# GpSimd takes the norm scalars, the weight quantisation and the split maxima of a four-layer gated transformer

## The chip, the core and the metric

The kernel runs as one program on one core of a Trainium2 chip. Its five engines run side by side and meet at semaphores: TensorE (PE: matrix products and transposes into the eight PSUM banks), VectorE (DVE), ScalarE (ACT), GpSimd (POOL, which also issues the indirect DMAs) and SyncE (SP, which issues most DMAs). The metric is the time of one execution on the device in microseconds, lower is better.

## The reference

Thirty-two positions `b` of 128 tokens and 128 channels pass four layers. Each layer adds an attention onto a context, and then a feed-forward part, both gated by a tanh and both fed with a layer norm of `x`:

```python
x = x + tanh(g_xattn[0]) * L0_xattn(_layernorm(x), ctx, ctx, ...)      # 16 heads of 8, biases
x = x + tanh(g_ffn[0])   * L0_ffn(_layernorm(x), w1, w2)               # bit-linear, gelu
x = x + tanh(g_xattn[1]) * L1_xattn(_layernorm(x), ctx, ctx, mask)     # one head of 128
x = x + tanh(g_ffn[1])   * L1_ffn(_layernorm(x), w_gate, w_up, w_down) # bit-linear, gated silu
x = x + tanh(g_xattn[2]) * L2_xattn(_layernorm(x), ctx, ctx, ...)      # 16 heads, shared key and value
x = x + tanh(g_ffn[2])   * L2_ffn(_layernorm(x), ...)                  # 8 experts, one per token
x = x + tanh(g_xattn[3]) * L3_xattn(_layernorm(x), ctx, mask, ...)     # 16 heads, masked
x = x + tanh(g_ffn[3])   * L3_ffn(_layernorm(x), ...)                  # butterfly transforms of 512

def _layernorm(x, eps=1e-05):
    m = mean(x); v = var(x)
    return (x - m) / sqrt(v + eps)

def _quant_weight(w):                                # both bit-linear layers, five weights in all
    s = clip(mean(abs(w)), EPS, None)
    return clip(round(w / s), -1.0, 1.0) * s         # used as it is; activations go to 8 bits
```

The attentions run along `b`-and-token pairs that the layouts in the kernel turn into 32 tiles of 128 rows; a softmax over 128 keys is taken for each of the 16 heads, with its true maximum.

## The kernel before

All of `x` stays in SBUF as 32 tiles of 128x128. The phases follow each other: attention L0, bit-linear F0, attention L1, bit-linear F1, attention L2, experts F2, attention L3, butterfly F3. Every engine has its own program, written out in the order in which it runs; no scheduler moves anything. An attention with 16 heads is a software pipeline over `t`: at iteration `t` PE makes the scores of tile `t` in both orientations (`pair_of_scores`, L1045 and L1048), DVE takes the maxima of tile `t+2` (L1487, two per tile), and ACT the exponentials (L753). The maxima of a tile are split into three bf16 parts (`nmax_parts`), transposed by PE (L1112), and subtracted again through a matrix product (L1517, L1059). In the attentions named in `SPLIT_BY_POOL` the four operations of that split are GpSimd's (`split_maxima`, L629 to L635), in the others DVE's (L1534, L1536, L1544, L1556). Four tiles are a quad; for each quad ACT writes normed tiles (`xn_quad`, L815), PE transposes them (L1123) and projects queries, keys and values (L1174, L1132, L1181), and ACT and DVE write copies masked to one head (`one_head_keys`, `one_head_queries`).

A norm has two stages. `tile_stats` (L1402) leaves the statistics of each tile in `stats` as soon as that tile of `x` is done. Between two phases DVE's `norm_stats` (L1410 to L1424) makes `mean`, `rstd` and `shift` for all 32 tiles at once, with a square root on ACT (`root`, L720) in the middle. Then the next phase's first `xn` can be written (L815, L858 or L1429). GpSimd has its own version, `norm_of` (L563 to L572), which takes the root as a power; it is used at the start of L0 and, quad by quad, for the routing.

Before either bit-linear phase DVE quantises its weights (`quantised_weights`, L1606 to L1617): for each weight a sum of magnitudes, a mean over the partitions by PE, a scale, and three passes over 128x512. PE then transposes the weights and DVE copies them (L1624) before the first tile can be quantised (L1641).

While L2 attends, the routing of F2 runs beside it. For each quad GpSimd makes the norms (L563 to L572) and the normed tiles (`late`, L659), PE transposes one tile per iteration (L1106) and makes the logits, DVE finds each token's expert and its rank, GpSimd adds the starts (L665 to L669) and scatters the four tiles to the experts' rows in HBM with four indirect DMAs in a row (`scatter`, L681). After L2 come the last quads' routing, F2 (its results go back with 40 indirect DMAs, L695), and then the residual additions (L1822) and statistics in four parts of eight tiles. `fill_wait` (L957) puts matrix products whose result nobody reads in front of a wait.

During L3 GpSimd multiplies butterfly matrices (`butterfly_step`, L614 and L619), three or four steps after each split.

## Time and profile before

| | |
|---|---|
| Median of 3 runs | 1155.06 us (1154.85 to 1159.28) |
| Profiled execution | 1164.92 us, its span 1163.2 us |
| PE, DVE, ACT, POOL busy in the span | 80%, 68%, 59%, 29% |
| Mean granted clock of PE | 0.904 |
| L0 / F0 / L1 / F1 | 0 to 250 / to 330.6 / to 386 / to 490 us |
| L2 / rest of the routing and F2 / residual | to 728 / to 850 / to 870 us |
| L3 / F3 | to 1092.5 / to 1163 us |

A row of a timeline gives the start, the busy time and the engine, then the line, the operation and its shape, "xN" for N instructions merged, and in brackets how long the engine sat idle before it and what ended that. SPq is the queue in which SP issues DMAs. "remote" is a release that the profile can't place.

### The profile page before, as it was taken

Reading aid. Unit: us, or ns where it says so; the run is one execution under the profiler, and the core shown is the slowest. Engines: PE = TensorE matmul, PEld = TensorE weight load, DVE = VectorE, ACT = ScalarE, POOL = GpSimd, SP = SyncE. Lnnn points to the kernel's source line nnn. Section 1 sums busy time; section 2 is a strip of 40 time slices with the busy share of each in tenths; the row PEclk is TensorE's granted clock in tenths of the full one; section 3 lists DMA queues with packets and bytes.
Section 4 is the critical chain, followed back from the end, with each engine's and each line's share of the span. In section 5 each row is a group of like instructions: output and inputs, shape, how many; then the busy total and the mean of one; then the engine's idle time right before and its main releaser. Section 6 shows DMA issues by size and latency. Waiting matters only on the chain.

```text
span 1163.2 us, 28810 instructions
## 1 busy us (share of the span) xinstructions
PE 934.0 (80%) x9421; PEld 556.2 (48%) x9431; DVE 786.8 (68%) x2141; ACT 688.1 (59%) x1474; POOL 334.5 (29%) x692
## 2 busy tenths in 40 slices
PE   3888998946656366599999986499929999999899
PEld 3644444423444233334554443277713454544598
DVE  3567777758989899848887872345583666667444
ACT  3556666528855466467777642065516777775466
POOL 5411111100000000001133344434413998777000
PEclk9999999976679677699999995599969999999899
DMA  6987655469995200000000000112130111111011
GB/s 181 157 108 52 49 42 43 37 152 202 181 180 76 72 1 1 1 1 2 2 10 12 11 18 21 31 54 57 56 100 19 57 39 56 54 52 47 3 34 36
DMA packets 285280, 67.04 MB, mean 58 GB/s; under 512 B 206241, under 2 KB 277985, under 8 KB 285154
## 3 DMA queue, kind: packets, MB, share of 16 engines
q1 hardware_dynamic: 279394, 50.94, 28.2%
q0 software_dynamic: 4896, 14.18, 3.7%
q8 instruction: 77, 1.26, 0.5%
q10 hardware_dynamic: 864, 0.27, 0.2%
q14 instruction: 49, 0.40, 0.1%
HBM read 34.80 MB, written 30.56 MB: 56 GB/s over the span
## 4 chain that ended last, share of the span: by engine, by line
PE 54%; DVE 28%; issue 6%; ACT 3%; DMA 3%; POOL 2%; SPq 1%; DVEq 1%; another core or an unknown queue 1%; ACTq 0%; POOLq 0%
PE bank L1045 14%; DVE nmax L1487 8%; PE bank L1077 6%; PE bank L1151 3%; PE bank L1333 3%; PE bank L1318 3%; DVE small L1661 3%; PE bank L1365 3%; PE bank L1059 2%; PE bank L1373 2%; DVE stats L1402 2%; DVE q_one L1653 2%; PE bank L1048 2%; DVE q_one L1690 2%; PE bank L1035 2%
## 5 line engine op out<-in xcount | busy, mean ns | idle before, releaser
L1487 DVE TENSOR_REDUCE nmax<-bank 128x8 f32<-128x1024 f32 x192 | 234.7, 1223 | 144.0 <-PE bank L1048 139.7
L753 ACT ACTIVATE probs_space<-bank 128x1024 f32<-128x1024 f32 x192 | 196.5, 1023 | 139.8 <-PE bank L1059 138.9
L1045 PE MATMUL bank<-q_one,k_all 32*128 32x512 f32 x768 | 216.8, 633 | 29.5 <-DVE nmax L1487 25.9
L1048 PE MATMUL bank<-k_one,q_all 32*128 32x512 f32 x768 | 214.2, 631 | 2.5 <-DVE nmax L1487 1.1
L1077 PEld LDWEIGHTS bank<-probs_space,vals 128*32 128x32 f32 x3072 | 73.6, 110 | 122.2 <-issue 121.6
L1077 PE MATMUL bank<-probs_space,vals 128*32 128x128 f32 x3072 | 126.3, 281 | 0.0
L563 POOL TENSOR_TENSOR var_b<-stats 128x4 f32<-128x4 f32 (+2 forms) x12 | 2.5, 208 | 356.7 <-DVE stats L1402 355.7
L1045 PEld LDWEIGHTS bank<-q_one,k_all 32*128 32x128 f32 x768 | 62.2, 185 | 58.6 <-issue 54.7
L761 ACT ACTIVATE k_one<-k_all,one_head 128x512 f32<-128x512 f32 x96 | 68.8, 722 | 20.1 <-DVE k_all L1507 18.6
L1059 PE MATMUL bank<-nmax_one,ones_bf 12*128 12x512 bf16 x384 | 78.1, 379 | 0.0
L1517 DVE TENSOR_TENSOR nmax_one<-bank,max_row 128x512 bf16<-128x512 bf16 x96 | 65.4, 681 | 3.6 <-PE bank L1112 3.6
L922 ACT ACTIVATE q_one<-bank,moe_b 128x128 f32<-128x128 f32 x160 | 45.8, 369 | 37.0 <-PE bank L1326 30.3
L629 POOL CAST nmax_parts<-nmax 128x16 bf16<-128x16 f32 x64 | 12.7, 198 | 184.5 <-DVE nmax L1487 184.4
L1402 DVE BATCH_NORM_STATS2 stats<-x 128x6 f32<-128x128 f32 x232 | 60.7, 286 | 5.9 <-DMA x<-in_x_dram 3.3
L957 PE MATMUL bank<-ones_bf 128*128 128x512 bf16 x125 | 38.4, 440 | 29.8 <-DVE stats L1402 24.0
L1048 PEld LDWEIGHTS bank<-k_one,q_all 32*128 32x128 f32 x768 | 58.7, 184 | 5.6 <-issue 4.5
L695 POOL DMA_INDIRECT token_rows<-q_one,slot_row_int x40 | 38.7, 967 | 64.7 <-DVE q_one L1800 64.3
L614 POOL TENSOR_TENSOR late<-bf_up,late 128x512 f32<-128x512 f32 x36 | 56.8, 1598 | 0.0
L1541 DVE RECIPROCAL o_inv<-bank 128x16 f32<-128x16 f32 x96 | 24.5, 255 | 44.5 <-PE bank L1156 36.6
L767 ACT ACTIVATE q_one<-q_all,one_head 128x512 f32<-128x512 f32 x80 | 54.5, 726 | 0.0
L875 ACT ACTIVATE q_one<-bank 128x1024 bf16<-128x1024 f16 x32 | 32.8, 1023 | 30.6 <-PE bank L1244 30.6
L942 ACT ACTIVATE q_one<-bank,up_bias 128x128 f32<-128x128 f32 x128 | 36.5, 368 | 18.7 <-PE bank L1365 18.7
(287 smaller groups left out, 2198.2 us busy)
## 6 DMA issues: line engine op xcount, KB each, us to landing
expert_rows<-zeros SPq DMA_DIRECT2D x8, 2128.5 KB, 32.0
late<-in_L_ffn_up_weights_dram POOLq DMA_DIRECT2D x9, 512.0 KB, 4.1
late<-_L_ffn_down_weights_dram POOLq DMA_DIRECT2D x9, 512.0 KB, 4.1
q_one<-expert_rows SPq DMA_DIRECT2D x40, 64.5 KB
q_scratch<-late SPq DMA_DIRECT2D x8, 256.0 KB
v_scratch<-moe_w SPq DMA_DIRECT2D x8, 256.0 KB, 3.1
vals<-v_scratch SPq DMA_DIRECT2D x8, 256.0 KB, 7.3
o_scratch<-o_tok SPq DMA_DIRECT2D x32, 64.0 KB, 3.4
```

What stands on the lines that cost most here:

```text
L614: pool.tensor_tensor(tmp(i), half(src, i % 2), weight, ALU.mult).then_inc(S("bf_step"), 1)
L753: act.activation(probs[:, 2 * g:2 * g + 2, :, :].rearrange("k g i q -> k (g i q)"), bank_pair[1][:, :, :].rearrange("k g f -> k (g f)"), A ...
L761: act.activation(k_one[:, c % 2, i, :], k_all[:, c % 2, :], ACT.Copy, scale=one_head[:, i:i + 1]).then_inc(S("t_k1"), 1)
L767: act.activation(q_one[:, c % 2, i, :], q_all[:, c % 2, :], ACT.Copy, scale=one_head[:, i:i + 1]).then_inc(S("t_q23" if i >= 2 else "t_q01 ...
L922: m = act.activation(hid2[:, t % 2, c * P:(c + 1) * P], bank[2 + t % 2][:, c * P:(c + 1) * P], ACT.Gelu_apprx_tanh, bias=moe_b1[:, bass.ds ...
L1045: pe.matmul(bank[2 + s], group(k_all, u, 2 * g + s), group(q_one, u, 2 * g + s), start=not masked, stop=False)
L1048: m = pe.matmul(bank[s], group(q_all, v, 2 * f + s), group(k_one, v, 2 * f + s), start=not masked, stop=True)
L1059: m = pe.matmul(bank[2 + s], ones_bf[first:last, :], nmax_one[first:last, u % 2, :, :], start=False, stop=True)
L1077: m = pe.matmul(bank[4][32 * j:32 * j + 32, g * P:(g + 1) * P], v[:, first:first + VW], probs[:, 2 * g + j // 2, j % 2 * 2 + s, :], start= ...
L1402: dve.bn_stats(stats[:, u, :], x[:, u * P:(u + 1) * P]).then_inc(S("stats"), 1)
L1487: dve.tensor_reduce(nmax[:, u % 2, 0, :].rearrange("q (g i) -> q g i", i=HG)[:, 2 * g:2 * g + 2, :], bank_pair[0][:, :, :].rearrange("q g ...
L1517: dve.tensor_tensor(nmax_one[:, (t + 1) % 2, :, :], over_blocks(bank[6][:, 3 * P:4 * P].bitcast(BF16)[:, 0:P], HG), max_row[:, :].unsqueez ...
```

## The change

1. `norm_stats` and `root` go. GpSimd's `norm_of` makes `rstd` and `shift` for groups of tiles, (0,8), (8,24), (24,32), and (0,4), (4,16), (16,32) for L3. Each user of a normed tile waits for the semaphore `norms` up to its tile.
2. The five bit-linear weights are loaded during L0 (`later_weights`, three more transfers), summed by DVE at the end of L0's iterations 10 to 14, scaled at 16, and quantised by GpSimd after its splits 19 to 23, three passes over 128x512 each.
3. In L2 too GpSimd splits the maxima, and two of the four `one_head_queries` of a quad move from DVE to ACT. Its routing work is spread over the iterations: norms of quad `c` after split `4c+8`, starts after `4c+14`, one scatter per iteration from 15 on.
4. L2's iterations -10 to -3 run between the last pairs of F1 on PE and ACT. The first quad uses bank 2, the fills go to bank 3, and L2's fills ahead of its first quads (9, 3, 3, 3) go. L3's start fill, 12 long, begins at the first residual addition.
5. Residual additions and statistics ahead of L3 come in parts (0,4), (4,8), (8,16), (16,24), (24,32), and L3's keys masked to one head wait for the first halves of them (`B_res`).

```diff
-        SPLIT_BY_POOL = ("L0", "L3")
-        STATS_BEFORE = {"L2": 5, "L3": 7}
-        NORMS = {"L2": 4, "L3": 5}
+
+        SPLIT_BY_POOL = ("L0", "L2", "L3")
         X_LEAD = 10
+
+        NORMS = {"F0": 0, "L1": NT, "F1": 2 * NT, "L2": 3 * NT, "L3": 4 * NT, "F3": 5 * NT}
+
+
+        SIZES_FROM, SCALES_IN, QUANTISED_FROM = 10, 16, 19
+
+        TENSOR_BETWEEN = {12: range(-X_LEAD, -5), 13: (-5,), 14: (-4, -3)}
+        SCALAR_BETWEEN = {11: range(-X_LEAD, -6), 12: (-6, -5), 13: (-4, -3)}
...
             def later_weights():
...
+                for i, name in enumerate(("L0_ffn_w1", "L0_ffn_w2", "L1_ffn_w_gate", "L1_ffn_w_up", "L1_ffn_w_down")):
+                    if i in (1, 4):
+                        sp.dma_start(quant_src[:, i, :], A[name]).then_inc(S("w_quant"), 16)
+                    else:
+                        sp.dma_start(quant_src[:, i, :].rearrange("p (c d) -> p c d", d=P),
+                                     A[name].rearrange("(c p) d -> p c d", p=P)).then_inc(S("w_quant"), 16)
...
+                if keep_scale:
+                    link(pool.tensor_tensor(var_a[:, at], var_a[:, at], keep[:, at], ALU.mult))
                 link(pool.tensor_scalar(rstd[:, at], var_a[:, at], 2.0, 0.0, ALU.mult, ALU.add), False)
                 link(pool.tensor_tensor(shift[:, at], mean2, var_a[:, at], ALU.mult))
+
+            def norms(stats_before, first, last, keep_scale=False):
+                pool.wait_ge(S("stats"), stats_before + last)
+                norm_of(first, last - first, keep_scale)
+                pool.sem_inc(S("norms"), last - first)
...
                     split_maxima(2 * NT, v)
+                    if v == 16:
+                        norms(7 * NT, 0, 8)
                     for _ in range(3 if k < 6 * STAGES else 4):
                         if k < 12 * STAGES:
                             butterfly_step(k)
                             k += 1
+                norms(7 * NT, 8, 24)
+                norms(7 * NT, 24, NT)
+
+            def quantised_weight(i):
+                own, inverse = quant_src[:, i, :], quant_inv[:, i:i + 1]
+                pool.wait_ge(S("wscale"), 1)
+                link(pool.tensor_scalar(own, own, inverse, MAGIC, ALU.mult, ALU.add))
+                link(pool.tensor_scalar(own, own, -MAGIC, 1.0, ALU.add, ALU.mult))
+                pool.tensor_scalar(quant_bf0[:, i, :] if i < 2 else quant_bf[:, i - 2, :], own, 1.0, -1.0,
+                                   ALU.min, ALU.max).then_inc(S("wq_ready"), 1)
 
             for v in range(NT):
                 split_maxima(0, v)
+                if v == 16:
+                    norms(NT, 0, 8)
+                if 0 <= v - QUANTISED_FROM < 5:
+                    quantised_weight(v - QUANTISED_FROM)
+            norms(NT, 8, 24)
+            norms(NT, 24, NT)
+            for layers in (2, 3, 4):
+                for first, last in ((0, 8), (8, 24), (24, NT)):
+                    norms(layers * NT, first, last)
             if "F2" in phases:
                 def norm_of_quad(c):
                     pool.wait_ge(S("stats"), NT * 5 + QT * (c + 1))
@@ -669,25 +701,32 @@
                     link(pool.tensor_tensor(dest[:, c % 2, :, :], dest[:, c % 2, :, :], hot[:, c % 2, :, :], ALU.mult))
                     pool.sem_inc(S("R_start"), 1)
 
-                def scatter(c):
+                def numbered(c):
...
                                    channel_multiplier=1, allow_small_or_imprecise_dtypes=True))
-                    pool.wait_ge(S("R_dest"), c + 1)
-                    for t in range(QT * c, QT * c + QT):
-                        pool.indirect_dma_start(
-                            out=expert_rows, out_offset=bass.IndirectOffsetOnAxis(ap=dest_int[:, t:t + 1], axis=0),
-                            in_=ring[:, t % ROUTE_RING, :], in_offset=None).then_inc(S(f"scattered_{c % 4}"), 16)
-
-                for c in range(NQ + 1):
-                    if c < NQ:
+
+                def scatter(t):
+                    pool.wait_ge(S("R_dest"), t // QT + 1)
+                    pool.indirect_dma_start(
+                        out=expert_rows, out_offset=bass.IndirectOffsetOnAxis(ap=dest_int[:, t:t + 1], axis=0),
+                        in_=ring[:, t % ROUTE_RING, :], in_offset=None).then_inc(S(f"scattered_{t // QT % 4}"), 16)
+
+                for v in range(NT + 4 * QT):
+                    if v < NT:
+                        split_maxima(NT, v)
+                    c = (v - 8) // QT
+                    if v % QT == 0 and live(c, NQ):
                         norm_of_quad(c)
-                    if c >= 1:
-                        rows_of_quad(c - 1)
-                        scatter(c - 1)
+                    c = (v - 14) // QT
+                    if v % QT == 2 and live(c, NQ):
+                        rows_of_quad(c)
+                        numbered(c)
+                    if live(v - 15):
+                        scatter(v - 15)
...
+            pool.wait_ge(S("wT_out"), 2)
+            for first, last in ((0, 4), (4, 16), (16, NT)):
+                norms(6 * NT, first, last, keep_scale=True)
...
                         past(act, "t_s1", 2 * (tiles + QT * (c - 1)))
+                        if layer == "L3" and c < 2:
+                            act.wait_ge(S("B_res"), (c + 1) * NT // 2)
...
+                        act.wait_ge(S("norms"), NORMS[layer] + u + 1)
                         act.activation(xn_quad[:, u % QT, :], x[:, u * P:(u + 1) * P], ACT.Identity,
                                        bias=shift[:, u:u + 1], scale=rstd[:, u:u + 1]).then_inc(S("t_xn"), 1)
...
+                    if next_iteration is not None and j in SCALAR_BETWEEN:
+                        if j == min(SCALAR_BETWEEN):
+                            act.wait_ge(S("bit_qx"), 2 * NP)
+                        for t in SCALAR_BETWEEN[j]:
+                            next_iteration(t)
...
-                    pe.wait_ge(S("stats"), NT * STATS_BEFORE[layer])
-                    if masked:
-                        pe.wait_ge(S("masks"), 1)
-                    fill_wait(9)
+                if layer == "L3":
...
+                    pe.wait_ge(S("B_res"), 1)
+                    fill_wait(12)
+
+                def quad_bank(c):
+
+                    return bank[2] if own and c == 0 else bank[5]
...
-                for t in iterations(layer):
+                def iteration(t):
                     u, w = t - lag, t - R_XT
                     routed = layer == "L2" and live(w)
+                    if layer == "L2" and t == -6:
+                        pe.wait_ge(S("bit_ge"), 2 * 2 * NP)
+                    if layer == "L2" and t == -3:
+                        pe.wait_ge(S("bit_hm"), 2 * NP)
+                    if layer == "L2" and t == 0:
+                        pe.wait_ge(S("stats"), NT * 5)
...
-                        if own and c == 0:
-                            fill_wait(3)
+                        if masked and c == 0:
+                            fill_wait(3, 3)
...
+                    if next_iteration is not None and j in TENSOR_BETWEEN:
+                        for t in TENSOR_BETWEEN[j]:
+                            next_iteration(t)
...
-            def norm_stats(n, n_stats=None, scale_by_keep=False):
-
-                dve.wait_ge(S("stats"), NT * (n_stats or n))
-                link(dve.tensor_tensor(var_a[:, :], stats[:, :, 2], stats[:, :, 5], ALU.add))
...
-                dve.sem_inc(S("var"), 1)
...
-                dve.sem_inc(S("norm"), 1)
-
             def normed(dst, u, name):
-                dve.tensor_scalar(dst, tile_of(x, u), column(mean, u), column(rstd, u), ALU.subtract,
-                                  ALU.mult).then_inc(S(name), 1)
+                wait(dve, "norms", NORMS[name.partition("_")[0]] + u + 1)
+                dve.tensor_scalar(dst, tile_of(x, u), column(rstd, u), column(shift, u), ALU.mult,
+                                  ALU.add).then_inc(S(name), 1)
...
+                    if not own and t == SCALES_IN:
+                        dve.wait_ge(S("wmean"), 1)
+                        link(dve.tensor_scalar(quant_scale[:, :], bank[7][:, P:P + 5], EPS, None, ALU.max))
+                        dve.reciprocal(quant_inv[:, :], quant_scale[:, :]).then_inc(S("wscale"), 1)
...
+                    i = t - SIZES_FROM
+                    if not own and 0 <= i < 5:
+                        dve.wait_ge(S("w_quant"), 16 * 5)
+                        link(dve.tensor_reduce(quant_sum[:, i:i + 1], quant_src[:, i, :], AX.X, ALU.add,
+                                               apply_absolute_value=True))
+                        if i == 4:
+                            dve.sem_inc(S("wsum"), 1)
...
-                dve.wait_ge(S("w_f0"), 32)
-                link(dve.memset(quant_sum[:, :], 0.0))
-                quantised_weights((0, 2), 1)
-                norm_stats(2)
                 bit_ffn("F0", False, 4)
...
-                for c in range(NT // GC):
-                    dve.wait_ge(S(f"chunk_in{c}"), 32)
-                    for t in range(c * GC, (c + 1) * GC):
+                for first, last in ((0, QT), (QT, GC), (GC, 2 * GC), (2 * GC, 3 * GC), (3 * GC, NT)):
+                    dve.wait_ge(S(f"chunk_in{first // GC}"), 32)
+                    for t in range(first, last):
                         dve.scalar_tensor_tensor(out=x[:, t * P:(t + 1) * P], in0=shared[:, t * P:(t + 1) * P],
                                                  scalar=gate[:, t:t + 1], in1=x[:, t * P:(t + 1) * P],
                                                  op0=ALU.mult, op1=ALU.add).then_inc(S("B_res"), 1)
-                    dve.wait_ge(S("B_res"), (c + 1) * GC)
-                    for t in range(c * GC, (c + 1) * GC):
+                    dve.wait_ge(S("B_res"), last)
+                    for t in range(first, last):
                         tile_stats(t)```

PE's program at the end of F1, first before and then of the change. L1226 (now L1300) is the last product of a pair of F1, L1244 (L1318) its transposes; `xn_quad`, `l_wq`, `l_wkv` and `k_one` are L2's.

```order
L1226 MATMUL bank<-ffn_wT,q_one 128x128 x8
L1244 MATMUL bank<-ident_half,q_one 128x128 x8
L1226 MATMUL bank<-ffn_wT,q_one 128x128 x8
L957 MATMUL bank<-ones_bf 128x512 x9
L1123 MATMUL bank<-ident,xn_quad 128x128 x4
L957 MATMUL bank<-ones_bf 128x512 x3
L1174 MATMUL bank<-xnT_quad,l_wq 128x512
L957 MATMUL bank<-ones_bf 128x512 x3
L1132 MATMUL bank<-contextT,l_wkv 128x512
L957 MATMUL bank<-ones_bf 128x512 x3
L1181 MATMUL bank<-l_wkv,contextT 128x128 x4
```

```order
L1300 MATMUL bank<-ffn_wT,q_one 128x128 x8
L1318 MATMUL bank<-ident_half,q_one 128x128 x8
L1186 MATMUL bank<-ident,xn_quad 128x128 x4
L1241 MATMUL bank<-xnT_quad,l_wq 128x512
L1300 MATMUL bank<-ffn_wT,q_one 128x128 x8
L1318 MATMUL bank<-ident_half,q_one 128x128 x8
L1195 MATMUL bank<-contextT,l_wkv 128x512
L1300 MATMUL bank<-ffn_wT,q_one 128x128 x8
L1248 MATMUL bank<-l_wkv,contextT 128x128 x4
L1004 MATMUL bank<-ones_bf 128x512 x8
L1101 MATMUL bank<-k_one,q_all 128x512 x2
```

The transposes and the query and key projections of L2's first quad now stand ahead of the last pairs of F1, and 18 fills are gone.

GpSimd's program in L2, between the norms of one quad and those of the next, before and then of the change (L659 and L691 write the normed tiles, L681 and L714 are the scatters, L640 to L646 the split):

```order
L571 TENSOR_SCALAR rstd<-var_a 128x4
L572 TENSOR_TENSOR shift<-twice_mean,var_a 128x4
L659 TENSOR_SCALAR late<-x,rstd,shift 128x128 x4
L665 COPY late<-late 128x8
L667 TENSOR_TENSOR late<-late 128x8 x4
L668 TENSOR_TENSOR late<-late 128x32
L669 TENSOR_TENSOR late<-late,hot 128x32
L677 IOTA late 128x4
L681 DMA expert_rows<-late,dest_int 33792x129 x4
L563 TENSOR_TENSOR var_b<-stats 128x4
```

```order
L577 TENSOR_SCALAR rstd<-var_a 128x4
L578 TENSOR_TENSOR shift<-twice_mean,var_a 128x4
L691 TENSOR_SCALAR late<-x,rstd,shift 128x128 x4
L714 DMA expert_rows<-late,dest_int 33792x129
L640 CAST nmax_parts<-nmax 128x4x4
L642 TENSOR_TENSOR nmax<-nmax,nmax_parts 128x16
L644 CAST nmax_parts<-nmax 128x4x4
L646 TENSOR_TENSOR nmax_parts<-nmax,nmax_parts 128x4x4
L714 DMA expert_rows<-late,dest_int 33792x129
L640 CAST nmax_parts<-nmax 128x4x4
L642 TENSOR_TENSOR nmax<-nmax,nmax_parts 128x16
L644 CAST nmax_parts<-nmax 128x4x4
```

The four scatters in a row have become one after each split, and the norms of a quad stand behind a split.

## Rows read from the trace of the kernel before

**Rows 1.** The page: share of the chain that ended last, by engine.

```profile
PE 54%; DVE 28%; issue 6%; ACT 3%; DMA 3%; POOL 2%; SPq 1%; DVEq 1%; another core or an unknown queue 1%; ACTq 0%; POOLq 0%
```

**Rows 2.** L3: busy time of PE, PEld, DVE, ACT, POOL; then DVE's maxima.

```profile
885.00:1085.00 200.00, 190.47 (x2954) 98.44 (x2954) 130.08 (x214) 140.59 (x237) 157.33 (x252) 1.00 0.13 44
...
L1487 DVE TENSOR_REDUCE nmax<-bank 128x8 f32<-128x1024 f32 x64 | 78.4, 1224 | 67.8 <-PE bank L1048 64.6 <-POOL nmax_parts L635 1.6 <-POOL nmax_parts L629 1.6
```

**Rows 3.** DVE's timeline from L0 into F0 (see above for its columns).

```profile
250.11 1.41 DVE L1606 TENSOR_REDUCE quant_sum<-late 128x1 f32<-128x512 f32 x2
...
257.77 0.76 DVE L1624 COPY ffn_wT<-bank 128x512 bf16<-128x512 bf16 x2 [0.15 <-DVE shift L1424]
```

**Rows 4.** DVE's timeline from F0 into L1.

```profile
330.62 0.22 DVE L1410 TENSOR_TENSOR var_a<-stats 128x32 f32<-128x32 f32 x1
...
333.09 0.60 DVE L1429 TENSOR_SCALAR xn<-x,mean,rstd 128x128 f32<-128x128 f32 x2
```

**Rows 5.** DVE's timeline from L1 into F1.

```profile
386.02 2.11 DVE L1606 TENSOR_REDUCE quant_sum<-late 128x1 f32<-128x512 f32 x3
...
395.70 1.09 DVE L1624 COPY ffn_wT<-bank 128x512 bf16<-128x512 bf16 x3 [0.15 <-DVE shift L1424]
```

**Rows 6.** PE's timeline from F1 into L2.

```profile
490.26 3.69 PE L957 MATMUL bank<-ones_bf 128*128 128x512 bf16 x9 [1.19 <-DVE stats L1402]
...
503.22 1.13 PE L1048 MATMUL bank<-k_one,q_all 32*128 32x512 f32 x4 [0.58 <-issue]
```

**Rows 7.** Waits in L2 (505 to 728): total us, times, longest us.

```profile
PE bank L1045 <- DVE nmax L1487: 12.1, 22, 1.7
...
DVE o_inv L1541 <- remote: 7.9, 4, 2.5
```

**Rows 8.** GpSimd's timeline in L2: the norms of a quad and its normed tiles.

```profile
624.00 0.21 POOL L563 TENSOR_TENSOR var_b<-stats 128x4 f32<-128x4 f32 x1 [2.28 <-DVE stats L1402]
...
627.48 1.75 POOL L659 TENSOR_SCALAR late<-x,rstd,shift 128x128 f32<-128x128 f32 x4
```

**Rows 9.** DVE's and PE's timelines in the same iteration of L2.

```profile
626.38 1.22 DVE L1487 TENSOR_REDUCE nmax<-bank 128x8 f32<-128x1024 f32 x1 [0.35 <-PE bank L1048]
...
630.78 0.27 PE L1106 MATMUL bank<-ident,late 128*128 128x128 f32 x1
```

**Rows 10.** All 40 of F2's returning indirect DMAs: min/median/max ns, start.

```profile
L695 POOL DMA_INDIRECT token_rows<-q_one,slot_row_int x40: 962/966/988, 760.3 to 848.3; - x40
```

**Rows 11.** GpSimd's timeline at the end of the routing: first and last of the late scatters.

```profile
732.32 1.10 POOL L681 DMA_INDIRECT expert_rows<-late,dest_int  x1 [0.94 <-DVE dest_int L1584]
...
744.32 0.97 POOL L681 DMA_INDIRECT expert_rows<-late,dest_int  x1 [0.30 <-issue]
```

**Rows 12.** DVE's and ACT's timelines ahead of L3, and GpSimd's power by size.

```profile
864.74 1.64 DVE L1402 BATCH_NORM_STATS2 stats<-x 128x6 f32<-128x128 f32 x8
...
875.68 0.49 ACT L815 ACTIVATE xn_quad<-x,shift,rstd 128x128 f32<-128x128 f32 x1 [1.21 <-PE bank L1123]
...
L570 POOL TENSOR_TENSOR var_a<-var_b,minus_half x12: 1017/1170/2269, 12.6 to 725.0; 128x4 f32<-128x4 f32 x9, 128x8 f32<-128x8 f32 x2, 128x12 f32<-128x12 f32 x1
```

**Rows 13.** GpSimd's timeline in L3.

```profile
992.90 0.20 POOL L629 CAST nmax_parts<-nmax 128x16 bf16<-128x16 f32 x1 [1.30 <-DVE nmax L1487]
...
993.91 1.55 POOL L614 TENSOR_TENSOR late<-bf_up,late 128x512 f32<-128x512 f32 x1
```

**Rows 14.** The chain of waits in L0, and SP's queue ahead of it.

```profile
94.22 4.10 SPq L407
...
60.36 4.58 SPq L377 DMA_DIRECT2D late<-in_L_ffn_w_dram  x1
64.99 0.50 SPq L379 DMA_DIRECT2D late<-in_L_ffn_w_dram  x1
```

**Rows 15.** DVE's timeline in L0: first maximum of two iterations that follow.

```profile
133.04 1.22 DVE L1487 TENSOR_REDUCE nmax<-bank 128x8 f32<-128x1024 f32 x1 [1.40 <-PE bank L1048]
...
138.30 1.23 DVE L1487 TENSOR_REDUCE nmax<-bank 128x8 f32<-128x1024 f32 x1 [0.75 <-PE bank L1048]
```

## What the change does to the time: the prediction

> **What bounds the kernel.** I read the page first, for who carries the chain: PE 54% and DVE 28%, and GpSimd 2% [rows 1]. So the kernel is a relay between PE and DVE. An instruction taken from DVE counts where the chain runs through DVE, and GpSimd is the engine with room. Then I read how full the stretches are. In L3 PE is busy 190.47 us of 200, GpSimd 157.33 [rows 2]: there GpSimd has little room left. Last I read the timelines of the five seams between phases, where DVE alone works and PE is idle [rows 3 to 6, 12], and the waits and GpSimd's timeline in L2 [rows 7 to 11].
>
> **L0 to F0: +7.3 us.** DVE begins the sums of the weights at 250.11 and reaches the copy of the transposed weights at 257.77 [rows 3]: 7.66 us of quantising and norms that all go. PE's transposes of the two weights and the last group's norm on GpSimd were hidden beside this and are now bare. I take 0.4 off, and keep 6 to 8.
>
> **F0 to L1: +0.5.** The norms take 333.09 - 330.62 = 2.47 us [rows 4], which go. But in L1 each of DVE's 32 tiles now waits for `norms` against a register before its `xn`. The trace has no such wait. DVE is the engine without a pause there, and by the smallest gaps between its instructions I put 0.06 us on each, 2 us in all. The ends are 0 and 0.1 us on each, so this seam gives between -0.7 and +2.5.
>
> **L1 to F1: +8.7.** The same as into F0, with three weights: 395.70 - 386.02 = 9.68 [rows 5], less 1.0 for three transposes that now stand alone. Between 8 and 9.7.
>
> **F1 to L2: +10.** Before, nine fills of 0.41 each begin only at 490.26, when the last statistics are there. The whole chain of quad 0 follows, and the first scores start at 503.22 [rows 6]. Now transposes and both projections of quad 0 stand ahead of the last products of F1. After the last product (1.19 before 490.26, so 489.1) PE has only the values' projection (0.6) and eight fills (8 x 0.41 = 3.3) to go, and starts scores at about 493.0. That is 10.2. The moved instructions have to fit into waits of PE and ACT between the last pairs; for what doesn't I take 0.2, and at worst 3. Between 7 and 11.
>
> **Inside L2: +3.5, the least certain term, made of three.**
> - DVE has four fewer operations in each tile and two fewer in each quad. PE's scores waited for DVE's maxima 22 times, 12.1 us in all [rows 7]. I take 7.5 of it, since the maxima themselves (1.22 each, two a tile) stay. Between 0 and +12.
> - Four times DVE waited for something that the profile can't place, 7.9 us in all, 2.5 at the longest [rows 7]; I found each of these beside the last of four scatters in a row, with PE and ACT idle as well. Spread out, the bursts are gone. F2 issues 40 single indirect DMAs of 962 to 988 ns each [rows 10]. I take +8, with 0 as the lower end and, for the case that every scatter brings such a wait, the first rival below.
> - The norms of a quad now stand behind a split on GpSimd. After the maximum of that iteration ends GpSimd needs 1.0 for the split (992.90 to 993.91, [rows 13]), 3.48 for the norms (624.00 to 627.48) and 0.44 for the first of four tiles [rows 8]: 4.9 us. PE asks for this tile in the next iteration, 630.78 - (626.38 + 1.22) = 3.2 us after the maximum [rows 9]. PE's instructions run in order, so everything behind L1106, the scores included, is late by 1.7, or 2.0 with the hops between the engines. Six quads have it while maxima run: -12. Between 0 (if the earlier relief is eaten up by this, the two overlap) and -15.
>
> **End of the routing: +3.** The last eight scatters took from 732.32 to 745.3 (744.32 + 0.97), in two bursts with the last quad's starts between them [rows 11]. The order at the end changes little, but normed tiles and starts are ready earlier. Between 0 and +7.
>
> **Into L3: +6.5.** Parts of eight tiles take 3.81 us on DVE, and the third ended at 866.38 [rows 12], so tile 16's statistics are there at 862.6. GpSimd needs for (4,16) about 2.31 (the 3.48 of four tiles less their power, 1.17) and 2.27 for the wider power [rows 8, 12]: 867.2. ACT wrote the first tile of the second quad at 875.68 [rows 12]; it can be 8 earlier. The key masks wait for 16 and 32 residual additions, which moves part of it back. Between 4 and 9.
>
> **GpSimd's norms in the middle of L3: -2.3.** At split 16 eight tiles' norms come in, about 3.9 us (3.48, and up to 0.5 for the wider power). GpSimd had at best 1.30 us of slack before a split [rows 13]. The rest, 2.6, delays a split, hence PE's L1112. Between -3 and 0. In L0 the same norms fit: a period is 138.30 - 133.04 = 5.26 us [rows 15], and a split and they take 4.9.
>
> **L3 to F3: +1.** The norms, 2.47 as in rows 4, go, but PE and ACT have weights of their own to prepare there. Between 0 and 2.5.
>
> **Loads and sums in L0: -4.5.** SP issues three more transfers ahead of the rows of L0 that it has to return. The two there took 4.58 and 0.50 us [rows 14], so three take 1.5 to 9.7. SP's issue of those rows is on the chain (L407, 4.10 at 94.22, [rows 14]). I take -2.5, nearer to the 0.50, since the 4.58 also holds a wait for a place in the queue. DVE's five sums cost 0.70 each (2.11 for three, [rows 5]), 3.5 in all; DVE sits idle 1.40 and 0.75 before its maxima [rows 15], which hides a part: -2, between -3.5 and 0. GpSimd's quantising is three passes over 512 columns; a pass lies between 0.44 (128 columns, [rows 8]) and 1.55 (two operands of 512 columns, [rows 13]), so 1.3 to 4.7 us behind a split of 1.0, in a period of 5.26. It is hidden, or at the upper end 0.4 too long five times.
>
> Against all work moved to GpSimd stands this: in L3, with GpSimd busy four fifths of the time, DVE's maxima last 1224 ns [rows 2], and 1.22 in L2 and L0 [rows 9, 15]. The Trainium skill (GPSIMD Engine Reference, Specifications) states that GpSimd shares its interfaces to SBUF with VectorE and that the two contend when DVE's instruction has two SBUF inputs. The maxima read PSUM, so this trace neither bears it out nor refutes it; by that rule each of the 15 passes of the quantising could hold DVE up once in L0, at most 15 x 1.55 = 23 us. Few of DVE's instructions in L0 have two inputs in SBUF, and no price for it is in the sum.
>
> **Sum.** 7.3 + 0.5 + 8.7 + 10 + 3.5 + 3 + 6.5 - 2.3 + 1 - 4.5 = 33.7 us. The profiled execution would fall from 1164.92 to 1131.2. That execution lies 9.86 above the median; taken off the median of 1155.06 the forecast is 1121.4, say 1122.
>
> **Rivals.**
> 1. *Slower: each scatter brings the unplaced wait.* If it comes of an indirect DMA's issue beside the pipeline and not of four in a row, 17 single scatters run inside L2's loop. At 2.5 each (the longest in rows 7) they cost 42.5, and the time is 1121.4 + 42.5 = 1164. It decides from 2.0 us a scatter. For: it appeared only beside scatters. Against: the wait came once for four of them, and F2's 40 single ones keep a steady length [rows 10]. 5%.
> 2. *GpSimd is late more often.* Its order is fixed, so a late norm delays splits, and a late split delays PE. If the stall on the normed tile costs 4 rather than 2 us (-12), and the loads in L0 cost 6.5 rather than 2.5 (-4), 1138. For: GpSimd goes from 2% of the chain to a link in each iteration of L2, and two waits for it show in L3 already [rows 2]. Against: it was busy only 29% of the whole span. 20%.
> 3. *More gain: the stall on the normed tile is not there.* PE asks for it 3.2 us after the maximum only in an iteration that runs undisturbed; if PE is behind anyway the 4.9 fit in: +12, 1110. 20%.
> 4. *No change.* Rival 1 at 2.0 us each, or rivals 1 and 2 in part: 1155. 3%.
>
> **How the numbers follow.** The forecast's case has 52%, its own range 1113 to 1131. For 8 in 10 the range takes in most of rivals 2 and 3, whose terms reach -12 and +12 and a few us more: 1103 to 1142. What a measurement can tell from no change is 0.5%, 5.8 us. Faster by more than that is 52 + 20 + 20 = 92%, within it 3%, slower 5%.
>
> **What the profile after would show.** Right: DVE goes from L0's last statistics to the weights' copy with no other work between; scores of L2 start within 4 us of F1's last product; no "remote" wait in L2; in its place PE's transpose of the normed tile (L1106 before) waiting for GpSimd some 2 us, six times; in L3 one late split near tile 16; the first masked maxima about 6 us sooner after the last residual. Wrong: "remote" waits at each scatter (rival 1); waits of PE for `nmax_parts` in L2 and a gap in L0's rows near 90 us (rival 2); no wait of that transpose (rival 3). The forecast fails if the seams give their 33 us but L2 itself becomes longer than before by more than 10.

## The result: 1167.6 us, slower, and the profile after

The change is slower, by 0.9%. Its median is 1167.6 us (1160.07 to 1174.18, 13 runs) against 1156.51 (1153.25 to 1161.19, 13 runs); the ratio is 1.0091, 95% interval 1.0066 to 1.0116. The forecast was 1122, its range 1103 to 1142, with 5% on slower.

The page of the changed kernel, its second section and the chain by engine, which answers to [rows 1]:

```profile
PEclk9998999995578777799998885589988999999999
...
PE 51%; DVE 22%; POOL 10%; issue 8%; ACT 3%; DMA 3%; SPq 2%; DVEq 1%; ACTq 0%; POOLq 0%
```

GpSimd has gone from 2% of the chain to 10%. DVE lost what it was meant to lose, 28% to 22%. PE's clock, in tenths of full speed by slice, falls to 8 in the second half of L2 (the three 8s in a row), where the kernel before has 9s throughout L2.

To see where the time went, I cut both executions at the starts of the first and the last maximum of each attention with 16 heads (DVE's line L1487, now L1542; 64 in each). "Half clock" is the time within the part at which PE had 1.2 GHz instead of 2.4.

| part | before, us | after, us | difference | forecast | half clock before / after |
|---|---|---|---|---|---|
| up to L0's first maximum | 52.1 | 52.6 | +0.5 | 0 | |
| L0 | 175.8 | 188.2 | +12.4 | +4.5 | 0 / 20 |
| L0's end, F0, L1, F1, L2's start | 276.5 | 249.4 | -27.1 | -26.5 | 140 / 140 |
| L2 | 190.5 | 215.7 | +25.2 | -3.5 | 0 / 27 |
| routing's end, F2, L3's start | 190.4 | 186.3 | -4.1 | -9.5 | 75 / 82 |
| L3 | 189.7 | 191.4 | +1.7 | +2.3 | 0 / 0 |
| rest of L3, F3 | 88.1 | 84.6 | -3.5 | -1.0 | 7.5 / 0 |
| span | 1163.2 | 1168.3 | +5.1 | -33.7 | |

(The difference of the medians is 11.1. The profiled execution of before lay 8.4 above its median, that of after 2.4, which is the other 6.)

Each part is read from one execution. How far such a reading carries shows in the kernels below that leave a part as it is in the change: L0 took 182.3 to 191.6 us in eight executions, with 7 to 31 us at half clock, and L2 212.5 to 222.3 in five, with 22 to 42. L3, with its full clock, took 191.2 to 191.7 in ten.

The seams gave what was forecast. First DVE's timeline of the changed kernel from L0 into F0, and then PE's from F1 into L2:

```profile
262.61 0.29 DVE L1477 BATCH_NORM_STATS2 stats<-x 128x6 f32<-128x128 f32 x1
262.82 0.74 DVE L1673 COPY ffn_wT<-bank 128x512 bf16<-128x512 bf16 x2
```

```profile
484.64 0.62 PE L1300 MATMUL bank<-ffn_wT,q_one 128*128 128x128 bf16 x8
485.59 1.13 PE L1248 MATMUL bank<-l_wkv,contextT 128*128 128x128 f32 x8 [0.34 <-ACT k_all L820]
486.56 1.89 PE L1004 MATMUL bank<-ones_bf 128*128 128x512 bf16 x8
488.97 1.13 PE L1101 MATMUL bank<-k_one,q_all 32*128 32x512 f32 x4 [0.52 <-issue]
```

The weights' copy follows the last statistics at once, where 7.66 us lay between them [rows 3]. L2's first scores start 3.7 us after F1's last product has ended (485.3); before it was 14.1 (489.1 to 503.22, [rows 6]).

The loss is inside L2 and L0. The waits from 490 to 735 us in the changed kernel (total, times, longest), to be read against [rows 7]:

```profile
PE bank L1098 <- DVE nmax L1542: 15.6, 18, 2.2
...
PE bank L1169 <- POOL late L691: 10.6, 6, 2.4
...
DVE late L1642 <- POOLq L702: 8.4, 5, 1.7
```

The second row is the wait I had forecast: six times, 1.8 on average. The third I had not. PE never waits here for `nmax_parts`, and no unplaced wait is left in L2. Here is one of each, PE's timeline of one quad, and DVE's:

```profile
645.97 2.05 PE L1248 MATMUL bank<-l_wkv,contextT 128*128 128x128 f32 x8
...
656.10 0.33 PE L1164 MATMUL bank<-ident,o_tok 128*128 128x128 f32 x1
658.06 0.46 PE L1169 MATMUL bank<-ident,late 128*128 128x128 f32 x1 [1.64 <-POOL late L691]
658.31 0.31 PE L1175 MATMUL bank<-ident_bf,nmax_parts 128*128 128x128 bf16 x1
658.42 2.02 PE L1195 MATMUL bank<-contextT,l_wkv 128*128 128x512 f32 x2
```

```profile
641.07 0.19 DVE L1642 TENSOR_REDUCE late<-late 128x4 f32<-128x32 f32 x1 [1.69 <-POOLq L702]
641.29 0.17 DVE L1643 CAST dest_int<-late 128x4 int32<-128x4 f32 x1
641.37 1.23 DVE L1542 TENSOR_REDUCE nmax<-bank 128x8 f32<-128x1024 f32 x1
```

DVE's L1642 adds up the rows of a quad, and it waits for the starts that GpSimd now makes behind a split. The next maximum stands behind it in DVE's order, and PE's scores behind that:

```profile
642.74 0.66 PE L1098 MATMUL bank<-q_one,k_all 32*128 32x512 f32 x1 [2.23 <-DVE nmax L1542]
```

After this wait and after the one at 658.06 PE works at half speed: the key projection at 658.42 takes 2.02 us, where it took 1.08 before. Two rows of PE's timeline of the kernel before, the second of them that projection:

```profile
177.06 0.66 PE L1045 MATMUL bank<-q_one,k_all 32*128 32x512 f32 x1 [1.50 <-DVE nmax L1487]
...
630.94 1.08 PE L1132 MATMUL bank<-contextT,l_wkv 128*128 128x512 f32 x2
```

Busy time and clock of three stretches of the changed kernel (duration, then PE, PEld, DVE, ACT, POOL, then the granted clock), the first while GpSimd is late, the second behind that wait, and the third behind an earlier wait of 2.24 us at 584.51:

```profile
655.00:658.00 3.00, 1.43 (x23) 0.51 (x17) 1.74 (x5) 1.31 (x3) 2.49 (x8) 1.00 0.00 0
658.50:661.80 3.30, 3.30 (x12) 1.04 (x12) 0.69 (x1) 1.66 (x4) 1.90 (x3) 0.54 0.09 25
```

```profile
584.60:588.00 3.40, 3.40 (x40) 2.36 (x40) 2.37 (x6) 1.02 (x1) 0.72 (x4) 1.00 0.00 0
```

So the half clock doesn't follow each wait. L2 has eleven waits of PE of 1.54 to 2.43 us; behind eight of them the clock fell, behind three (1.69 at 543.65, 2.24 at 584.51, 1.65 at 598.25) it stayed full.

The working claim was: GpSimd hands over late twice in each quad of L2, and PE pays once by waiting and mostly once more by working at half clock. L0's 12.4 us would be of the same kind, with SP's loads and DVE's sums as what is late. The chain of waits in L0 has the start of it, a row of L0 that comes back late, and PE at half clock behind it (such a product takes 0.66 at full clock); then SP's timeline from the first bit-linear weight on, and PE's:

```profile
80.63 6.21 DMA o_scratch<-o_tok
...
89.69 1.19 PE bank L1098
```

```profile
60.90 4.60 SPq L388 DMA_DIRECT2D late<-in_L_ffn_w_dram  x1
65.55 0.50 SPq L386 DMA_DIRECT2D late<-in_L_ffn_w_dram  x1
66.09 0.43 SPq L388 DMA_DIRECT2D late<-in_L_ffn_w_gate_dram  x1
66.56 0.51 SPq L388 DMA_DIRECT2D late<-in_L_ffn_w_up_dram  x1
67.11 0.50 SPq L386 DMA_DIRECT2D late<-in_L_ffn_w_down_dram  x1
...
80.63 4.14 SPq L417 DMA_DIRECT2D o_scratch<-o_tok  x2
```

```profile
88.69 0.48 PE L1164 MATMUL bank<-ident,o_back 128*128 128x128 f32 x1 [3.48 <-DMA o_back<-o_scratch]
```

In the kernel before SP issued that row 3.5 us earlier:

```profile
77.16 3.01 SPq L407 DMA_DIRECT2D o_scratch<-o_tok  x2
```

### The profile page after: what moved, and what is told of

The parts are those of the page before. It is cut to its first block, busy times and chain, and to the rows that moved or that the text cites. A ratio compares the mean times of both kernels' runs of the same rounds, so it can differ in the third digit from the quotient of the medians.

```text
span 1168.3 us, 29084 instructions
## 1 busy us (share of the span) xinstructions
PE 959.3 (82%) x9404; PEld 570.5 (49%) x9414; DVE 749.8 (64%) x1924; ACT 689.8 (59%) x1478; POOL 444.2 (38%) x1018
## 4 chain that ended last, share of the span: by engine, by line
PE 51%; DVE 22%; POOL 10%; issue 8%; ACT 3%; DMA 3%; SPq 2%; DVEq 1%; ACTq 0%; POOLq 0%
PE bank L1098 12%; DVE nmax L1542 6%; PE bank L1130 5%; PE bank L1214 3%; PE bank L1408 3%; PE bank L1393 3%; DVE small L1711 3%; PE bank L1448 2%; PE bank L1440 2%; POOL late L625 2%; PE bank L1112 2%; DVE q_one L1703 2%; PE bank L1223 2%; DVE stats L1477 2%; DVE q_one L1740 2%
## 5 line engine op out<-in xcount | busy, mean ns | idle before, releaser
L1542 DVE TENSOR_REDUCE nmax<-bank 128x8 f32<-128x1024 f32 x192 | 235.1, 1224 | 161.0 <-PE bank L1101 157.8
L1098 PE MATMUL bank<-q_one,k_all 32*128 32x512 f32 x768 | 226.2, 659 | 34.3 <-DVE nmax L1542 29.6
L1101 PE MATMUL bank<-k_one,q_all 32*128 32x512 f32 x768 | 221.7, 652 | 2.5 <-DVE nmax L1542 1.2
L1130 PE MATMUL bank<-probs_space,vals 128*32 128x128 f32 x3072 | 129.0, 288 | 0.0
L640 POOL CAST nmax_parts<-nmax 128x16 bf16<-128x16 f32 x96 | 19.0, 198 | 289.0 <-DVE nmax L1542 284.9
L1098 PEld LDWEIGHTS bank<-q_one,k_all 32*128 32x128 f32 x768 | 64.2, 192 | 66.8 <-issue 63.7
L567 POOL TENSOR_TENSOR var_b<-stats 128x8 f32<-128x8 f32 (+3 forms) x30 | 6.8, 227 | 230.1 <-DVE stats L1477 190.4
L806 ACT ACTIVATE q_one<-q_all,one_head 128x512 f32<-128x512 f32 x96 | 64.2, 726 | 0.0
L1477 DVE BATCH_NORM_STATS2 stats<-x 128x6 f32<-128x128 f32 x232 | 60.9, 287 | 4.7 <-DMA x<-in_x_dram 2.0
L1101 PEld LDWEIGHTS bank<-k_one,q_all 32*128 32x128 f32 x768 | 60.5, 190 | 5.7 <-issue 4.6
L574 POOL TENSOR_TENSOR var_a<-var_b,minus_half 128x8 f32<-128x8 f32 (+3 forms) x30 | 52.6, 1752 | 2.3
```

Source lines behind the costliest of these rows:

```text
L574: link(pool.tensor_tensor(var_a[:, at], var_b[:, at], minus_half[:, 0:n], ALU.pow))
L806: act.activation(q_one[:, c % 2, i, :], q_all[:, c % 2, :], ACT.Copy, scale=one_head[:, i:i + 1]).then_inc(S("t_q23" if i >= 2 else "t_q01 ...
L1098: pe.matmul(bank[2 + s], group(k_all, u, 2 * g + s), group(q_one, u, 2 * g + s), start=not masked, stop=False)
L1101: m = pe.matmul(bank[s], group(q_all, v, 2 * f + s), group(k_one, v, 2 * f + s), start=not masked, stop=True)
L1130: m = pe.matmul(bank[4][32 * j:32 * j + 32, g * P:(g + 1) * P], v[:, first:first + VW], probs[:, 2 * g + j // 2, j % 2 * 2 + s, :], start= ...
L1477: dve.bn_stats(stats[:, u, :], x[:, u * P:(u + 1) * P]).then_inc(S("stats"), 1)
```

## The experiments

All times are ratios to the kernel before on the same chip, since chips differ by about 1%. The change itself wasn't timed again on those chips. "L2" is the time from L2's first to last maximum in the profiled execution, and "L0" likewise. The expectations of the L2 part undone, of both early edits, of the waits filled and of the sums moved counted to the 61st of the 64 maxima instead: 205.9 us in the change, 182.3 before, 180.4 with the part undone. I give both where they are needed.

**The L2 part undone.** GpSimd's loop of L2 is again the one before:

```diff
-        SPLIT_BY_POOL = ("L0", "L2", "L3")
+        SPLIT_BY_POOL = ("L0", "L3")
...
+                for c in range(NQ + 1):
+                    if c < NQ:
+                        norm_of_quad(c)
+                    if c >= 1:
+                        rows_of_quad(c - 1)
+                        numbered(c - 1)
+                        for t in range(QT * (c - 1), QT * c):
+                            scatter(t)
```

> The change with its part in L2 undone: DVE splits the maxima, GpSimd makes norms, starts and four scatters in a row quad by quad as before; the seams and L0 stay changed. Theory (hand-overs of GpSimd inside L2 stall PE, and PE's clock falls after each): L2 from its first maximum (490.2) to its last takes the 182.3 us of before instead of 205.9, so the time is 23 us below the change, about 1144. Rival (L2 is longer because it starts out of F1's tail, with its fills gone): L2 stays at 200 us or more and the time near 1167.

Measured: ratio 0.9775 (0.9726 to 0.9823), L2 188.6 us (180.4 to the 61st maximum). The rest of the change alone is worth 2.2%, and the loss is in the part on L2. That L2 starts out of F1's tail is no cause.

**Norms one iteration earlier.**

```diff
-                    c = (v - 8) // QT
-                    if v % QT == 0 and live(c, NQ):
+                    c = (v - 7) // QT
+                    if v % QT == 3 and live(c, NQ):
                         norm_of_quad(c)
```

> The change with one edit: in L2 the norms of quad c stand behind split 4c+7 instead of 4c+8, one iteration before PE transposes the first normed tile. Theory (two stalls per quad, the norms' 1.6 to 2.4 us on PE and, after it, 3.4 us of PE at half its clock): six times (2.0 + 1.7) = 22 us at most, if the clock falls only for this stall; with the starts' stall left, 12 to 20 us are gained, 1148 to 1156. Rival (the single scatters or a shared port slow L2): not more than 3 us gained, since both stay as they are.

**Starts one iteration earlier.**

```diff
-                    c = (v - 14) // QT
-                    if v % QT == 2 and live(c, NQ):
+                    c = (v - 13) // QT
+                    if v % QT == 1 and live(c, NQ):
                         rows_of_quad(c)
```

> The change with one edit: in L2 the starts of quad c (five adds, a product, the row numbers) stand behind split 4c+13 instead of 4c+14, so that DVE's reduction of that quad's rows no longer waits for them. Theory: DVE waited for them 8.4 us in 5 times and PE for the next maxima 2.2 each; 8 to 12 us are gained, 1156 to 1160. Rival (the single scatters): nothing, since they stay where they are.

**Both.**

> The change with both edits in L2: norms of a quad behind split 4c+7, starts behind split 4c+13. Theory (the two late hand-overs with the clock's fall after each are all that L2 lost): L2 from first to last maximum takes 180 to 183 us as with the part undone (180.3), ratio to the kernel before 0.975 to 0.980. Rival (single scatters, or GpSimd beside DVE on a shared port, slow the rest): L2 stays over 186 us and the ratio near that of either edit alone, 0.984.

Measured, ratio and L2: norms early 0.9841 (0.9797 to 0.9885), 197.4 us; starts early 0.9848 (0.9808 to 0.9887), 203.2; both 0.9709 (0.9673 to 0.9744), 184.3. From 215.7, the one edit takes 18.3, the other 12.5, together 31.4 (to the 61st maximum 176.2 are left, where 180 to 183 were expected). The two losses add up, and they are more than all that L2 lost against the kernel before. The two single edits gained more than I expected: 1148 to 1156 and 1156 to 1160 were expected, and their ratios are 1138 and 1139 us on the chip of the change. L2's own gains are about as expected. The part behind L2 also became shorter, from 186.3 us to 179.8 and 177.7 (the end of the routing, below). With both, PE's only large wait in L2 is the old one for the maxima, and its clock there is full; the waits, and the stretch from 486.2 to 670.5 with its clock as last figure but two:

```profile
PE bank L1098 <- DVE nmax L1542: 7.1, 18, 0.9
```

```profile
486.20:670.50 184.30, 175.09 (x1918) 90.45 (x1916) 133.08 (x272) 139.64 (x252) 77.64 (x266) 1.00 0.03 8
```

GpSimd does the same 77 us of work here as in the change (77.13). So its load wasn't the trouble; its place was.

**The waits filled.** The GpSimd hand-overs stay late, and PE gets work whose result nobody reads:

```diff
+                    if layer == "L2" and t > 12 and quad(t, 3) is not None:
+                        pe.wait_ge(S("t_kn"), quads + quad(t, 3) + 1)
+                        fill_wait(8, 5)
                     pair_of_scores(t, 0, t + 2, 1)
...
+                    if routed and quad(t, 5) is not None:
+                        pe.wait_ge(S("t_qa"), quads + quad(t, 5) + 1)
+                        fill_wait(6, 5)
                     if routed:
                         pe.wait_ge(S("R_xn"), w + 1)
```

> The change, with PE made busy in L2's two waits: six products into bank 5 whose result nobody reads ahead of the wait for a quad's normed tiles, and eight ahead of the scores behind the wait for its starts. Theory (each wait costs PE twice, once idle and once in 3.4 us at half its clock): the waits stay, the windows at half clock inside L2 (8 of them, 1.7 us each) go, and L2 takes 8 to 13 us less than 205.9, ratio to the kernel before 0.998 to 1.003. Rival (the clock falls for another reason, or what counts are the waits alone): the windows stay and the time rises by the fills, up to 10 us.

Measured: ratio 0.9962 (0.9938 to 0.9986), a little better than expected. L2 took 205.9 us instead of 215.7 (to the 61st maximum 195.2 instead of 205.9). Of its 27 us at half clock 6 are left, which by halves makes 10.7 us, against 9.8 measured:

```profile
484.80:690.70 205.90, 192.24 (x1980) 96.40 (x1978) 133.88 (x271) 140.19 (x252) 77.96 (x266) 0.99 0.02 7
```

This shows the second half of the price. GpSimd is still late (DVE's wait for the starts is 8.5 us in 5 times, PE's for the normed tile 4.2 in 6, the rest of it now filled), and with the clock mostly kept up this costs the rest, 21.6 us over both early edits.

**Scatters four in a row again,** with both early edits:

```diff
-                    if live(v - 15):
-                        scatter(v - 15)
+                    if v % QT == 3 and live(v - 15):
+                        for t in range(v - 15, v - 15 + QT):
+                            scatter(t)
```

> As with both edits, and the scatters again four in a row, behind the split 4c+15. Theory that the unplaced wait comes of four indirect DMAs in a row: the 'remote' waits of 2 to 2.5 us come back, four or more of them, and with the clock's fall L2 is 8 to 15 us longer than with both edits. Rival (they came of something else that the change removed): the time is that of both edits within 3 us.

Measured: ratio 0.9887 (0.9851 to 0.9923), L2 205.5 us, so four in a row cost 21 us over single ones, where 8 to 15 were expected. The reason is mostly another than expected. PE's longest waits, and GpSimd ahead of one of them:

```profile
PE bank L1176 <- POOL nmax_parts L646: 13.0, 4, 3.9
```

```profile
590.61 1.26 POOL L714 DMA_INDIRECT expert_rows<-late,dest_int  x1 [0.20 <-issue]
...
595.67 0.20 POOL L640 CAST nmax_parts<-nmax 128x16 bf16<-128x16 f32 x1
```

Four indirect DMAs take 5.1 us of GpSimd behind the normed tiles, and the next split is late by them. PE is at half clock for 24 us of this L2. Unplaced waits did come back, DVE's 4.7 us once and ACT's 4.6 in three. Spreading the scatters is thus needed once GpSimd splits, and it is not itself what slowed L2.

**DVE splits, the routing spread and early.**

```diff
-        SPLIT_BY_POOL = ("L0", "L2", "L3")
+        SPLIT_BY_POOL = ("L0", "L3")
...
-                        split_maxima(NT, v)
+                        pool.wait_ge(S("t_mx"), 2 * (NT + v + 1))
```

> Both early edits, but in L2 DVE splits the maxima and writes two of the masked queries as before, while GpSimd's routing stays spread, one scatter per tile, paced by the maxima. It prices the split by itself and asks where the unplaced waits come from. Theory (the split on GpSimd relieves DVE, worth some 4 of the 7.5 us that I had put on it, and the unplaced waits belong to four scatters in a row): L2 takes 186 to 190 us instead of 184.3, with no 'remote' wait. Rival (the unplaced waits come with DVE's own splits, whatever the scatters): four or more of them, 2 to 3 us each on DVE or ACT, as with the L2 part undone, and L2 188 us or more.

Measured: ratio 0.9710 (0.9668 to 0.9752), L2 188.5 us. The split on GpSimd, with the two masked queries on ACT, is worth 4.2 us of L2. Neither L2 has any half clock, and with all edits L2 again took 184.5, so 4.2 is more than such readings differ by; the ratio of the whole, with intervals of 0.4%, can't tell it. Waits of this kernel in L2:

```profile
PE bank L1098 <- DVE nmax L1542: 12.5, 19, 1.9
...
ACT o_heads L840 <- remote: 1.2, 1, 1.2
```

With the bursts, in the kernel before and with the part undone, the unplaced waits of ACT were 12.3 and 11.7 us; here they are 1.2. They show in the kernels with four scatters in a row and are all but gone in those without. Yet L2 takes 188.6 with them (the part undone) and 188.5 without, so no cost of them shows. The two kernels differ in the whole order of GpSimd's routing, so that this isn't a test of the waits alone.

**L0: loads later.**

```diff
-                for i, name in enumerate(("L0_ffn_w1", "L0_ffn_w2", "L1_ffn_w_gate", "L1_ffn_w_up", "L1_ffn_w_down")):
...
+                ffn_weights((0, 1))
...
+                    if t in (5, 6, 7):
+                        ffn_weights((t - 3,))
```

> The change with one edit: F1's three weights are loaded at iterations 5, 6 and 7 of L0 instead of with the others at iteration 1. Theory (SP's queue of loads delays the first rows of L0, and PE at 88 us then runs three windows at half its clock): tiles 4 to 8 of L0 come 5 to 7 us earlier against the change, 1161 in all. Rival (the three sums and the longer queue of the other loads are the cause): under 2 us.

**L0: loads at 3 to 5, sums moved.**

```diff
+                    if t in (3, 4, 5):
+                        ffn_weights((t - 1,))
...
-                    i = t - SIZES_FROM
+                    i = {8: 0, 9: 1, 10: 2, 12: 3, 13: 4}.get(t, -1)
```

> The change, with F1's weights loaded at iterations 3 to 5 of L0 and DVE's five sums at the ends of iterations 8, 9, 10, 12 and 13, so that none stands ahead of DVE's k_all at a quad's start (11 did). Theory (a sum there makes PE wait 2.2 us and then run at half its clock for 3.4): L0's last maxima come 3 to 5 us earlier than with the loads alone moved (229.7), ratio 0.999 to 1.001. Rival (the sums cost 0.7 each wherever they stand): 229.7 stays, ratio 1.003.

Measured: loads later 1.0037 (1.0014 to 1.0060), L0 185.7 us; both 1.0029 (1.0006 to 1.0051), L0 181.8. With the loads later tile 8's maximum comes 43.0 us after the first instead of 49.5 (42.7 in the kernel before). This holds beyond one execution: it came after 45.5 to 51.1 us in the nine kernels with these loads at iteration 1, and after 42.7 to 43.0 in the four with them later. Of the 6.5 us 4 are given back later: PE still has 17 us at half clock in L0, and a load now holds SP's queue there, here in that kernel:

```profile
91.66 4.59 SPq L387 DMA_DIRECT2D late<-in_L_ffn_w_gate_dram  x1
96.30 1.75 SPq L421 DMA_DIRECT2D o_scratch<-o_tok  x1
```

So a load of F1 holds SP for 4.6 us there, in front of a row that L0 needs back; two of the three do so at iterations 3 to 5 (4.13 and 4.63 us). Moving the sums shortens the wait of PE for which they were moved, from 2.22 us (at 139.04 in the change) to 1.50 (at 135.35). L0 became 3.9 us shorter by it, with 3 us at half clock instead of 17; the 61st maximum came at 226.3 instead of 229.7, as expected. Whether the moved sums did all of that isn't shown, since L0 unchanged took 182.3 to 191.6 us. The ratio, 1.0029, missed the expected 0.999 to 1.001.

**Sums left out.**

```diff
-                        link(dve.tensor_reduce(quant_sum[:, i:i + 1], quant_src[:, i, :], AX.X, ALU.add,
-                                               apply_absolute_value=True))
+                        if i == 0:
+                            link(dve.memset(quant_sum[:, :], 400.0))
```

> The change with loads and sums moved, and DVE's five sums of magnitudes left out (the scales come from a constant). It prices what is left of the sums in L0, which takes 181.8 us from first to last maximum with them and 175.8 in the kernel before. Theory (a sum of 0.70 on DVE shows in full wherever DVE has no wait, and DVE bounds L0 half the time): 2.5 to 3.5 us less, about 179. Rival (they are hidden now, and the norms and GpSimd's quantising make up the 6): less than 1 us.

Measured (one run, no interval): L0 181.3 us against 181.8. Tiles 11, 12, 13 and 16 come 0.5 to 0.8 us sooner behind the tile ahead of them, 2.6 us in all, and tile 23 by 1.3; tiles 14, 15, 26 and 27 come 0.5 to 1.4 later, with 7 us at half clock instead of 3. I can't say from this what is left of the sums. Of the last 6 us of L0, 1.7 are the 3 us at half clock; the rest stays open. One piece that I overlooked stands in every changed kernel: at iteration 16 DVE makes the scales (L1560, L1561) ahead of `k_all`, and PE waits 1.91 us at that quad's start, where it waited 1.50 before; no run here tests it.

**Norms behind the last split.**

```diff
-                    if v == 16:
-                        norms(7 * NT, 0, 8)
...
+                norms(7 * NT, 0, 8)
                 norms(7 * NT, 8, 24)
```

> The change, with the norms of tiles 0 to 7 that stand at split 16 of L0 and of L3 moved behind the last split of each, where GpSimd has nothing else. Theory (they delay one split, and PE waits): L3 from first to last maximum falls from 191.4 to 189.6, L0 by 1 to 2.5, and neither next phase starts later; ratio to the kernel before 1.005 to 1.007. Rival (the first normed tile is then late for F0 or F3): the phases behind take back 2 to 4 us, ratio 1.009 or more.

Measured: 1.0011 (0.9992 to 1.0030), below the expected 1.005 to 1.007. L3 took 189.5 us instead of 191.4, as expected, and the rest of L3 and F3 took 86.2 us, as in four kernels without this edit (86.0 to 86.2, all with 3 us at half clock there; 84.6 where there is none). L0 didn't gain (188.3). L3's 1.9 us are 0.2% of the whole; the other 0.6% under the change's 1.0091 I can't place. So a difference of that size between ratios from different chips isn't safe to read, and the two L0 kernels above (1.0037 and 1.0029) differ from 1.0091 by no more.

**All of it.**

> All edits together: in L2 norms behind split 4c+7 and starts behind 4c+13, F1's weights at iterations 3 to 5 of L0, the sums at 8, 9, 10, 12 and 13, the norms behind the last splits. Theory (the losses are separate, each a wait of PE with its fall of the clock): ratio 0.971 of both early edits, less 0.006 for L0 and 0.003 for the norms: 0.960 to 0.964, 1112 to 1120. Rival (they overlap): 0.968 or more.

Measured: ratio 0.9644 (0.9618 to 0.9670), 1125.62 us where the kernel before took 1167.64. L2 takes 184.5, L3 189.6, L0 183.6. It is the fastest of all, just above what was expected (0.960 to 0.964): L0 was 2.5 us shorter than with both early edits alone (186.1), not 6.

## Why the prediction was wrong

**The seams held.** From L0's end to L2's start the change gave 27.1 us for 26.5. By the same rows as in [rows 3 to 6], L0 to F0 gave 7.8, F0 with L1 0.3, L1 to F1 9.6 and F1 to L2 9.2, each within 1 us of its term: what DVE does alone between two phases went nearly in full. The other signs of the forecast came true as well: first scores within 4 us of F1's last product, no unplaced wait in L2, six waits for the normed tile, one late split in the middle of L3 (PE waits 1.41 us at 1003.64). So did the sign that it would fail: the seams held and L2 became longer by more than 10 us.

**The step that failed is "Inside L2: +3.5".** All three of its terms were off, and one was missing.
- The late normed tile was there, six times, as forecast, at 1.8 us for 2.0. But I priced only the wait. With the half clock behind it, it cost 18.3 us, not 12 (norms early: PE's 10.6 us of waits go, and 16 us at half clock, which by halves makes 8).
- The starts were missing altogether. I had put them among GpSimd's moved work ("starts after `4c+14`") and never asked who waits for them. DVE does, at the end of the same iteration, with the maxima queued behind it: 12.5 us (starts early). The prediction's own rule of naming what is queued behind a waiting instruction was applied to PE and not to DVE.
- The relief of DVE was 4.2 us, not 7.5 (DVE splits).
- The unplaced waits of 7.9 us were taken as +8, and no gain from their going shows: L2 is as long with them as without (188.6 and 188.5). A wait that a profile shows on DVE and ACT need not be time on the path.

With both hand-overs early, L2 gains 6.2 us over the kernel before (6.2 less 18.3 and 12.5 is -24.6, against the -25.2 measured). So the term's size was in reach, and its sign came from two places in an order.

**"End of the routing: +3" failed by the same hand-over.** From the start of L2's last maximum to the end of the last scatter the kernel before took 50.4 us and the change 51.9; with both early edits it took 43.6. The three stretches, in the columns as above:

```profile
694.90:745.30 50.40, 28.83 (x190) 17.23 (x188) 18.46 (x83) 9.64 (x22) 28.31 (x67) 0.57 0.08 26
```

```profile
705.90:757.80 51.90, 32.90 (x190) 19.00 (x188) 18.43 (x82) 9.86 (x22) 30.59 (x72) 0.50 0.08 25
```

```profile
670.50:714.10 43.60, 22.61 (x192) 13.76 (x191) 19.70 (x84) 9.59 (x22) 30.56 (x72) 0.69 0.09 30
```

In the change the last late starts make PE wait 2.23 us at 704.68, and its clock is at half from 705.90 on for 61 us; with both early edits it falls only 17 us behind L2's last maximum. The five kernels with early starts took 43.6 to 46.6 us here. Of the seven with late starts five took 51.9 to 52.2, but two took 42.7 and 45.7, so a late hand-over makes the early fall likely and doesn't force it. This is most of what the early edits gained beyond L2.

**"Loads and sums in L0: -4.5" was mis-sized**, at 12.4 (11.2 as the mean of the eight executions of this L0, 6.5 to 15.8). The three loads themselves took SP only 0.43, 0.51 and 0.50 us, less than my 2.5; the 4.60 is the first weight's load, which was there before. But loads behind them took longer too, and SP issued L0's row 3.5 us later (80.63 for 77.16). PE waited 3.48 us for it, and 10 us at half clock followed: tile 8 was 6.8 us late. A sum at iteration 11 stood ahead of DVE's k_all, and PE waited 2.2 us instead of 1.5. In all PE had 20 us at half clock in L0, some 10 of the 12.4, and the clock was in none of my terms. I had argued that DVE's idle time hides part of the sums; with them left out 2.6 of their 3.5 us went where they had stood, and came back elsewhere (one run).

**"Into L3: +6.5"** was nearly right: from the end of the last statistics to the first masked maximum 9.7 us (882.57 to 892.23) instead of 15.2 (870.14 to 885.35), so +5.5. DVE's rows, of before and then of the change:

```profile
868.50 1.64 DVE L1402 BATCH_NORM_STATS2 stats<-x 128x6 f32<-128x128 f32 x8
...
885.35 1.23 DVE L1487 TENSOR_REDUCE nmax<-bank 128x8 f32<-128x1024 f32 x1 [12.61 <-PE bank L1048]
```

```profile
880.93 1.64 DVE L1477 BATCH_NORM_STATS2 stats<-x 128x6 f32<-128x128 f32 x8
892.23 1.23 DVE L1542 TENSOR_REDUCE nmax<-bank 128x8 f32<-128x1024 f32 x1 [9.66 <-PE bank L1101]
```

ACT writes the second quad's first tile 0.6 us before the last statistics are begun, where I had 1.3 (867.2 and 868.50):

```profile
880.32 0.49 ACT L855 ACTIVATE xn_quad<-x,shift,rstd 128x128 f32<-128x128 f32 x1 [4.74 <-POOLq L583]
```

What is missing of the 9.5 for that part is thus the end of the routing (-1.5 for +3); F2's 40 returning DMAs took 88.0 us from the first to the last in every kernel. **"GpSimd's norms in the middle of L3: -2.3"** was right (1.7, and it goes with the norms moved), though its own working gives 2.6. The end gave 3.5 instead of 1, but the kernel before had 7.5 us at half clock there and the change none, which by halves is 3.7: no gain from the norms shows in it.

**Of the rivals**, the first, a stall at each scatter, was wrong though its time was near: no unplaced wait came with the single scatters. The second named the mechanism, GpSimd late more often and SP's loads, and priced it at 16 us with 20%. Its sign in L0, the gap near 90 us, came (3.48 us at 88.69); its sign in L2, waits for `nmax_parts`, didn't. It was this kind of loss, at more than twice the price (the profiled execution missed the forecast by 38.8 us), because it left out the clock and the starts. The cost of a late hand-over has to be worked out as wait plus half clock. Within L2 13.7 us went to the clock behind its eleven waits, 1.2 on average and at least 1.7 where it fell; by the average the six forecast waits of 2.0 would have been 12 + 6 x 1.2 = 19 us.

## What to carry to other kernels

When work moves to an engine with room, its place in that engine's order can decide more than its length: for each product ask which instruction waits for it, in which iteration, and what is queued behind that instruction. Here two blocks moved by one iteration turned a loss of 0.9% into a gain of 2.9%, with GpSimd as busy as before. On PE, price a wait of about 2 us twice, once as idle time and once for the slow stretch that mostly followed it here; where the wait can't be removed, filling it gave the second part back. A wait in a list of waits counts only if the chain runs through it. And cut several executions of the same part before reading a few microseconds in one: here a part with such waits differed by 9 to 10 us between executions, a part without them by half a microsecond.

## What the runs showed of the hardware

- In the loops of L0 and L2 PE had its full clock throughout before (granted clock 1.00). In the change it worked at 1.2 GHz for a while behind eight of the eleven waits of 1.54 to 2.43 us in L2 (27 us in all), and for 20 us in L0. The length of the wait alone doesn't decide it: 2.24 us at 584.51 had nothing behind it, while one of L0's three waits of 1.50 had (at 189.21), and in the kernel before none of five of 1.50 (the one at 177.06 among them) nor one of 1.73 us. The Trainium skill (TensorE: Matmul & The Clock Gate, Part 1: The HAM clock gate) has PE's clock fall to 1.2 GHz after idle time. These runs agree in so far as the half clock in L2 went with the waits (27 us to none with both early edits) and, with the waits filled, to 6.
- With identical instructions there, the part from L2's last to L3's first maximum took 186.3 us in the change and 177.1 with only the loads of L0 moved, by where PE's clock fell (82 and 58 us at half clock). The 9 us lie in the end of the routing (51.9 and 42.7 us), whose 190 products kept PE busy for 32.9 and 22.6 us. The changed kernel's spread of 14 us over 13 runs, against 8 for the kernel before, is of that size; that it comes from this isn't shown.
- GpSimd's passes over 128x512 with one operand took 0.61 to 0.69 us on average, nearer to the lower end of 0.44 to 1.55 that I had. With 78 us of GpSimd's work in L2 beside DVE instead of 53, DVE's maxima lasted 1224 ns instead of 1220 and its statistics 292 in both: no contention that costs time shows. Few of DVE's instructions there have two inputs in SBUF, so this isn't a test of that case.
